# Cross-attention probabilities split before their transpose, turned by a DMA, and multiplied on 128 rows

## What is computed

```python
ln_out = _ln(layernorm(x), ln_w, ln_b)
q  = _ln(fp8_linear(ln_out, wq))        # 16 heads of 128, in 8 groups of 2
k, v = _ln(fp8_linear(ln_out, wk)), fp8_linear(ln_out, wv)     # 8 groups
core = gqa(q, k, v)                     # softmax over 256 tokens
qx = _ln(fp8_linear(ln_out, wqx))
kx, vx = split(cond @ w_kv_x.T)         # 64 context tokens, kx normalised
xout = gqa(qx, kx, vx)                  # softmax over 64 context tokens
y = fp8_linear(concat(core, xout), wproj)
x = x + tanh(g_xattn) * y
x = x + tanh(g_ffn) * moe(layernorm(x)) # 8 experts, top 2, and a shared one
```

## Time and profile before

| | us |
|---|---|
| median of 3 runs | 1148.06 |
| lowest and highest | 1147.09, 1149.56 |
| span of the profiled execution | 1146.5 |

### The profile page before, as it was taken

One profiled execution on the slowest core, in us unless ns is written; L12 is line 12 of the kernel. 1 busy time (PEld: TensorE's weight loads), 2 busy tenths in 40 slices (PEclk: granted clock), 3 DMA queues, 4 the chain that ended last, 5 costly groups with the idle time before them and its releaser, 6 DMA issues.

```text
span 1146.5 us, 22682 instructions
## 1 busy us (share of the span) xinstructions
PE 1045.5 (91%) x7648; PEld 751.5 (66%) x7648; DVE 916.7 (80%) x1807; ACT 766.1 (67%) x2441; POOL 698.6 (61%) x533
## 2 busy tenths in 40 slices
PE   1567999998999999899899989999999999999998
PEld 0355677776776777677677767777776556555554
DVE  8898899998998999899899989998999683333332
ACT  2466878877887888788788878778877542222222
POOL 4776777677676857776586767777674242222222
PEclk9867899999999999999999999999999999999999
DMA  9321000000000000000000000000002110000000
GB/s 257 95 74 37 1 2 2 1 2 1 0 0 1 0 0 0 1 0 0 1 0 0 0 1 0 0 1 0 0 19 67 55 52 20 1 17 2 0 18 18
DMA packets 17409, 21.45 MB, mean 19 GB/s; under 512 B 1360, under 2 KB 15024, under 8 KB 17344
## 3 DMA queue, kind: packets, MB, share of 16 engines
q1 hardware_dynamic: 13232, 18.67, 5.1%
q0 software_dynamic: 4112, 2.10, 1.3%
HBM read 20.76 MB, written 2.10 MB: 20 GB/s over the span
## 4 chain that ended last, share of the span: by engine, by line
DVE 51%; issue 20%; PE 12%; ACT 12%; POOL 4%; DVEq 0%; DMA 0%; ACTq 0%; POOLq 0%
DVE nmx L1001 8%; DVE yb L1058 8%; DVE pT L1010 6%; DVE ss L1033 5%; POOL pT L1410 4%; ACT raw L700 4%; DVE var L1044 3%; DVE ss L1042 3%; ACT prob L741 3%; ACT yb L759 2%; DVE qT L1027 2%; ACT sq L699 2%; DVE stage L966 2%; DVE yb L1055 2%; PE S L351 2%
## 5 line engine op out<-in xcount | busy, mean ns | idle before, releaser
L1320 POOL TENSOR_TENSOR rstd<-var,mhalf 128x8 f32<-128x8 f32 (+1 forms) x128 | 176.5, 1379 | 205.4 <-DVE var L1037 202.1
L314 PE MATMUL A<-w_hi,xq 128*128 128x256 f16 (+1 forms) x1024 | 186.7, 251 | 39.9 <-ACT raw L700 21.5
L1372 POOL TENSOR_TENSOR raw<-raw,rstd 128x1024 f32<-128x1024 f32 (+1 forms) x128 | 185.9, 1452 | 10.0
L741 ACT ACTIVATE prob<-S,nmx 128x256 f32<-128x256 f32 x256 | 119.0, 470 | 107.4 <-DVE nmx L1001 107.3
L315 PE MATMUL A<-w_lo,xq 128*128 128x256 f16 (+1 forms) x1024 | 182.9, 251 | 0.0
L1410 POOL TENSOR_TENSOR pT<-zq,pT 128x512 f16<-128x512 f32 (+1 forms) x56 | 65.2, 1166 | 172.8 <-ACT pT L843 164.5
L314 PEld LDWEIGHTS A<-w_hi,xq 128*128 128x128 f16 x1024 | 101.9, 100 | 63.9 <-ACT raw L700 24.8
L848 ACT ACTIVATE qT<-A 128x512 f32<-128x512 f32 (+1 forms) x56 | 33.4, 596 | 146.4 <-PE A L308 146.3
L1360 POOL TENSOR_TENSOR prob<-prob,rl 128x1024 f32<-128x1024 f32 x64 | 121.2, 1893 | 16.2 <-DVE rl L1050 16.2
L341 PE MATMUL S<-kT,qT 128*128 128x256 f32 x512 | 122.5, 382 | 1.3 <-ACT kT L721 1.0
L1001 DVE TENSOR_REDUCE nmx<-S 128x2 f32<-128x512 f32 (+1 forms) x192 | 114.1, 595 | 8.1 <-PE S L351 8.1
(11 more groups left out here) (190 smaller groups left out, 2828.5 us busy)
## 6 DMA issues: line engine op xcount, KB each, us to landing
stage<-wallT SPq DMA_DIRECT2D x8, 1024.0 KB, 4.9
wp<-wpT POOLq DMA_DIRECT2D x1, 2048.0 KB, 30.6
out<-v_lo SPq DMA_DIRECT2D x8, 256.0 KB, 2.2
xs<-x SPq DMA_DIRECT2D x1, 1792.0 KB, 20.9
sq<-w2s SPq DMA_DIRECT2D x7, 128.0 KB, 3.0
sq<-w1T SPq DMA_DIRECT2D x3, 256.0 KB, 2.8
sq<-w3T SPq DMA_DIRECT2D x3, 256.0 KB, 3.1
raw<-w1T SPq DMA_DIRECT2D x3, 256.0 KB, 2.8
```

Of the source, the lines that this page charges most:

```text
L314: nc.tensor.matmul(o, l, w_hi[:, c, col:col + n], start=(c == 0), stop=False)
L741: last = nc.scalar.activation(prob[:, p, j, :], o[:, t * S:(t + 1) * S], ACT.Exp, bias=nmx[:, p, j:j + 1], accum_out=lsum[:, p, j:j + 1])
L1320: return nc.gpsimd.tensor_tensor(dst, src, mhalf[:, 0:n], ALU.pow)
L1372: nc.gpsimd.tensor_tensor(raw[:, p, u, :], raw[:, p, u, :], rstd[:, p, u].rearrange("p (u o) -> p u o", o=1).to_broadcast([P, w, D]), ALU. ...
```

## The change

The cross probabilities are split into their halves before the transpose, while they still lie in SBUF with tokens on the rows. ACT writes the high half of `probx` into `pxs[:, p, j, 0, :]` (`high_px`), DVE the low half into `pxs[:, p, j, 1, :]` (`low_px`), so that each of the four blocks j has 64 high columns and 64 low columns beside each other. SP then issues one DMA transpose (`flip`) of 128 x 512 float16 from `pxs` to `pxT`, after which rows 0 to 63 of `pxT` hold the high half and rows 64 to 127 the low half, with 512 columns. `pv_cross` becomes two matmuls of 512 columns: the context's high v, stored twice (rows 0 to 63 and 64 to 127), on all 128 rows, which gives high by high and high by low at once, and the low v on the first 64 rows. PE's `transpose_px` is gone, the half in the next tick too, and bank T0 is used once less in a tick.

ACT's part moves: `high_px` stands between `read_kv` and `high_p(…, 0)`, ahead of where `high_p(…, 2)` was. DVE's `low_px` stands where `low_p(…, 2)` was. The context is stored doubled for all sequences at the start, so the four copies of `front_cx` are gone. `front_xq`, the last scaling of the front, is split in two: kinds 0 and 1 (q) stand where it was, kinds 2 and 3 (k and v) stand after the last maxima. SP now issues 60 of the 64 flips ahead of and between the loads of the feed-forward part.

```diff
+                def high_px(n, p, half):
+                    done(act, g_norm, n)
+                    if live(n - 2):
+                        act.wait_ge(ld_px[p], half * 16)
+                    nc.scalar.activation(pxs[:, p, :, 0, :], probx[:, p, :, :], ACT.Copy, scale=PSCALE).then_inc(a_px, 1)
...
+                def low_px(n, p):
+                    done(dve, a_px, n)
+                    nc.vector.scalar_tensor_tensor(pxs[:, p, :, 1, :], probx[:, p, :, :], PSCALE, pxs[:, p, :, 0, :], ALU.mult,
+                                                   ALU.subtract).then_inc(d_px, 1)
...
+            def flip(n):
+                p = n % 2
+                done(sp, d_px, n)
+                done(sp, mm_xo, n - 2)
+                sp.dma_start_transpose(pxT[:, p, :, :], pxs[:, p, :, :, :].rearrange("p j k c -> p (j k c)")).then_inc(ld_px[p], 16)
...
-                def pv_cross(n, p, vg, t):
+                def pv_cross(n, p, vg):
...
+                    pe.wait_ge(ld_px[p], (b * (G // 2) + (g - 4) // 2 + 1) * 16)
+                    done(pe, a_core, n)
+                    both = pxT[:, p, :, :].rearrange("p j s -> p (j s)")
+                    nc.tensor.matmul(VB[:, :], vx_hi[:, vg, :], both, start=True, stop=False)
+                    nc.tensor.matmul(VB[:, :], vx_lo[0:SC, vg, :], both[0:SC], start=False, stop=True).then_inc(mm_xo, 1)
...
+                    done(act, d_px, n - 2)
...
                 if live(n0): read_kv(n0, par(0))
+                if live(n0 - 3): high_px(n0 - 3, par(3), b * (G // 2) + (g - 3) // 2)
                 if live(n0 - 3): high_p(n0 - 3, par(3), 0)
...
                 if between and g == G - 1:
-                    done(dve, mm_kv, n0)
-                    front_xq(b + 1)
-                if live(n0 - 3): low_p(n0 - 3, par(3), 2)
+                    done(dve, mm_q1, n0)
+                    front_xq(b + 1, 0)
+                if live(n0 - 3): low_px(n0 - 3, par(3))
...
                     if g == G - 1:
-                        done(dve, mm_x, n0)
-                        front_cx(b + 1)
+                        done(dve, mm_kv, n0)
+                        front_xq(b + 1, 2)
```

125 lines of the change are left out of this document (57 added, 68 removed).

## The result

The changed kernel takes 1156.32 us (median of 6 runs, 1155.53 to 1158.08), the one before 1147.76 (6 runs, 1147.09 to 1149.56). The ratio is 1.007, with a 95% interval of 1.0057 to 1.0082: slower by 8.6 us. The forecast was 1159 in a range of 1142 to 1166. The number is near.

What follows compares the result with a forecast made beforehand. The prediction took DVE and ACT's circle, not PE, as the bound. Terms +11.0 (high_px), +2.5 (low_px), -1.6 (front_xq) and -1.0 (drain and startup) sum to +10.9 on 1148.06: 1159 us, range 1142 to 1166.

Steps and rivals of the forecast that it cites:

- What bounds the kernel: Loop: a repeating circle of DVE and ACT sets the 12.33 us tick; PE, busy 91%, waits 0.42 us for DVE.
- PE, 0 in the loop: Loop: fewer transposes and half of pv_cross's matmul time shorten nobody's wait; 0, at most 38 us if PE set the pace.
- Drain and startup, -1.0, between -3 and +2: Outside the loop: shorter pv_cross in the drain gains 1.0; startup's PE gain is set against the doubled context.
- ACT's `high_px`, +11.0: Loop: low_p(…, 0) comes 0.11 us late, so POOL goes ahead of DVE's L1055; 0.25 us in each of 44 ticks.
- The bound of "no flip", +4.8: Lower bound of the high_px term: DVE-POOL order does not turn, POOL is only held back 0.11 us in 44 ticks.
- DVE's `low_px`, +2.5: On the circle, replacing low_p(…, 2): 0.04 us more in each of 62 ticks, from -3 to +6; DVE beats POOL's L1372.
- `front_xq`, -1.6: Once a sequence, ahead of the last maxima: splitting the scaling saves 0.2 us for each of 8.
- The flip, 0: SP's DMA transposes: free up to 12 us of landing; load_up(2) behind the last flip in the drain costs 0, at most +2.
- Rival A: Loop: the port order does not turn; +4.7, 1153; chance 0.13 at 1151 to 1154, 0.12 for its "no change".
- rival C: Loop: POOL's L1372 on k catches low_px, costing DVE about 0.8 us in each of 60 ticks; +48, 1207; chance 0.07.
- if L1058 still takes 2.0, A or B holds: Sign in the changed profile: DVE's L1058 still the long instruction, where the forecast had its mean fall from 1515 towards 430.
- B: Rival for the loop: banks and PE matter after all, DVE's q reads and scores never late; -5.6, 1142; chance 0.17.

Runs made afterwards that it cites:

- e6: Changed kernel with low_px moved behind the next tick's two read_q and the first flip behind the startup's loads; drain loads still behind flips: 1147.34 us.
- e8: Changed kernel with the edits of e1, e2 and e6 joined (the first flip's move too): 1136.33 us, ratio 0.9892 to the kernel before.
- e1: Changed kernel with ACT's high_px moved behind scale_out(…, 0), in front of high_p(…, 1): 1153.9 us, ratio 1.0049 to the kernel before.
- e11: Changed kernel with PE's work given back where it was taken, by repeating transposes of q and of the probabilities' second half: 1162.97 us.
- e7: Changed kernel with the two matmuls of pv_cross issued twice in each step: 1168.78 us, ratio 1.0176 to the kernel before.
- e4: Changed kernel with a second ACT instruction like high_px right behind it, into a tile nobody reads: 1181.19 us, ratio 1.0281 to the kernel before.
- e5: Kernel before with only an ACT instruction of 256 elements from probx, into an unread tile, added ahead of high_p(…, 0): 1154.12 us, ratio 1.0048.
- e2: Changed kernel with the drain's feed-forward weight loads put ahead of the flips they stood behind in SP's queue: 1153.03 us, ratio 1.0045 to the kernel before.
- e9: Kernel before with only the doubled context and the split front_xq: 1147.24 us, ratio 0.9989 to the kernel before.

## Why the prediction came out near, step by step

- **What bounds the kernel.** Right: DVE and ACT's circle, PE waiting for DVE. e6 and e8 show it most directly: 0.29 us taken off the circle bring 0.16 to 0.35 in six of the eight ticks, and nothing in g = 2 and 6 (e8 against e1).
- **PE, 0 in the loop.** Right for an ordinary tick at the places it was taken from (e11, 0.01 a tick, though its loop as a whole is 2.6 us longer). That it holds at any place was wrong (e7, 0.20 a tick).
- **Drain and startup, -1.0, between -3 and +2.** Wrong, and outside its bounds: +2.7 behind the loop and +2.2 to +4.6 ahead of it. In the drain I followed the flips past `load_up(2)` alone, the load behind the last of them. `load_down(0)` stands behind the flip of step 60 and is needed first; it was enough to ask of each load in the queue what it now stands behind. In the startup I had the doubled context in (0.7), and took a shorter PE for a gain that did not come; what the runs show in its place is one tick in which the lower clock fell behind the output projection in six of the nine traces with the change and in none of the four without (0.9 to 2.6 us). Why is open.
- **ACT's `high_px`, +11.0.** The slip was right (0.10 at `low_p(…, 0)`), the price of a turned order too (0.24 in e4, 0.25 in e5). The count was wrong, and this is the term that missed by most: 44 dear ticks at 0.25 were forecast. The clip comes 0.07 late, not 0.11, which puts it within 0.02 us of POOL, and there DVE still wins most, 5 lost in the changed kernel's trace, none in e2's. Undoing the slip is worth 2.4 in the medians (3.8 in the loops of the two traces). The bound of "no flip", +4.8, had the right price but too many ticks: 0.10 to 0.11 in three of the eight ticks of a sequence (e1), which is 2.2 for the 21 of them.
- **DVE's `low_px`, +2.5.** Its duration is that of `low_p(…, 2)`, 0.37: 0. That DVE wins against POOL's multiplication of k was right in ordinary ticks. I had not asked whom DVE then holds up: POOL, by 0.14 (0.97 in place of 0.83). Whether the 0.25 in every g = 4, 1.7 in all, come from that is open, as e6 and e8 show. The +2.5 is thus shown by no run.
- **`front_xq`, -1.6.** Right in kind, 2.1 in e9's g = 7; the 0.9 in the medians is within the noise.
- **The flip, 0.** Right: 2.4 us to land, and no wait for it in the loop. The rows of queue 1 on the two pages (packets, MB, share of 16 engines' span), before and changed, put 8.8% of 1156.3 less 5.1% of 1146.5 = 43 us on 64 flips, 0.68 each:

```profile
q1 hardware_dynamic: 13232, 18.67, 5.1%
```
```profile
q1 hardware_dynamic: 48048, 27.06, 8.8%
```

  The 0.4 us that I had worked out from the Trainium skill's rate (Advanced Engine Details and Errata, "X-Bar Transpose (TRN2)") is of that order for the moving itself, and a sixth of the time to landing; SP alone spends 1.2 us on the issue.

The sum of the loop was 11.9 and measured 3.0; startup and drain were -1.0 and measured 6.8 in the trace. Two errors of opposite sign made a good number: that it came out near is luck. Rival A (no turned order) is the better account of the loop, though its 1153 is no nearer; rival C did happen, but in g = 7 alone, once in the changed kernel's trace:

```profile
159.13 0.41 DVE L932 TENSOR_SCALAR xq<-zq 128x1024 f16<-128x1024 f16 x1
159.46 1.05 DVE L1011 SCALAR_TENSOR_TENSOR pxs<-probx,pxs 128x256 f16<-128x256 f32 x1
```

Of the signs named in the prediction, "if L1058 still takes 2.0, A or B holds" was met in 28 of the 56 ticks, down from 42.

In the 14 that it lost the clip is caught in 5 and the variance of k in 9 (the seven g = 4, and twice g = 0).

Open: what moves the clip by the few nanoseconds that decide, and how often it falls to POOL over many executions; what makes g = 4 dear; what sends the lower clock behind the output projection in the startup. Nor is settled what lengthens the last tick of the startup by 0.5 to 0.6 us.

## What to carry to other kernels

When a DMA joins a queue, list every load behind it with the time at which its reader needs it; the last one is not always the first one missed. When an operation becomes one that shares a port, ask both who can catch it and whom it catches, and follow the second one to the end of the next tick. And place a new instruction by the circle, not by data flow: `low_px` in its first place cost the change its gain; behind the reads of q, with the two other repairs, the kernel is 11.6 us faster than the one before.
